# Laying 160 channels as 128 and 32 in a four-layer cross-attention kernel, with the 32-row products issued beside the scores

## The reference

```
q = x @ Wq;  k = ctx @ Wk;  v = ctx @ Wv          # 160 channels = 20 heads x 8
p = softmax(q k^T / sqrt(8))                       # 20 heads, 128 x 77
x = x + (p v) @ Wout + bias
```

## Time and profile before

| | us |
|---|---|
| median of 3 runs | 2361.54 (2361.36 to 2363.28) |
| the profiled execution | 2364.91 |
| its span, first to last instruction | 2363.1 |
| TensorE busy | 2177.9 (92%) |
| TensorE weight loads busy | 1807.6 (76%) |
| VectorE busy | 1397.6 (59%) |
| ScalarE busy | 1076.6 (46%) |
| GpSimd busy | 459.0 (19%) |
| mean granted TensorE clock | 0.968 of full |

### The profile page before, as it was taken

The page is one execution under the profiler, slowest core; times in us unless marked ns, Lnnn a source line. Parts: engine busy times, 40 slices in busy tenths (PEclk is TensorE's granted clock), DMA queues, the critical chain, the costliest instruction groups (busy, mean ns, idle before and its releaser), DMA issues. The chain is left out here.

```text
span 2363.1 us, 74795 instructions
## 1 busy us (share of the span) xinstructions
PE 2177.9 (92%) x26394; PEld 1807.6 (76%) x26394; DVE 1397.6 (59%) x4195; ACT 1076.6 (46%) x2733; POOL 459.0 (19%) x870
## 2 busy tenths in 40 slices
PE   1699999999999999999999999999999999999976
PEld 1578787788788778878878887887878778888765
DVE  3236666566566566656656665665666566566554
ACT  0244444445445444544544454454455445444431
POOL 0012212221121211221212121122122112221210
PEclk9799999999999999999999999999999999999985
DMA  2111111111111111111111111111111111111000
GB/s 85 49 46 37 51 48 36 46 48 44 37 50 43 37 50 49 39 42 49 44 37 50 45 39 46 50 42 40 49 44 37 50 43 42 45 50 35 24 10 5
DMA packets 92280, 101.21 MB, mean 43 GB/s; under 512 B 37313, under 2 KB 68505, under 8 KB 91898
## 3 DMA queue, kind: packets, MB, share of 16 engines
q1 hardware_dynamic: 90220, 92.86, 14.1%
q10 hardware_dynamic: 1678, 3.33, 0.5%
HBM read 34.13 MB, written 5.41 MB: 17 GB/s over the span
## 5 line engine op out<-in xcount | busy, mean ns | idle before, releaser
L1056 DVE TENSOR_REDUCE top<-ps_s 128x6 f32<-128x462 f32 (+3 forms) x1024 | 514.7, 547 | 186.9 <-PE ps_s L687 184.2
L954 ACT ACTIVATE p_t<-ps_s 116x512 f32<-116x512 f32 (+1 forms) x768 | 370.3, 544 | 68.8 <-PE ps_s L714 68.5
L1096 DVE TENSOR_TENSOR weighted<-ps_k,probs 128x462 f32<-128x462 f32 (+1 forms) x256 | 143.2, 559 | 328.7 <-PE ps_k L784 325.2
L687 PE MATMUL ps_s<-k_blocks,q_sb 32*128 32x231 f32 (+1 forms) x3584 | 296.5, 377 | 16.0 <-issue 15.9
L759 PE MATMUL ps_c<-p_t,v_rows 116*27 116x128 f32 (+1 forms) x7168 | 285.0, 282 | 14.2 <-DMA v_rows<-v_img 11.7
L1272 POOL TENSOR_TENSOR k_blocks<-k_sb,mask_k 128x231 f32<-128x231 f32 x384 | 211.6, 572 | 426.5 <-PE ps_s L714 411.5
L759 PEld LDWEIGHTS ps_c<-p_t,v_rows 116*27 116x27 f32 (+1 forms) x7168 | 212.1, 108 | 84.9 <-issue 49.1
L827 PE MATMUL ps_c<-o_t,wo 128*80 128x128 f32 x2048 | 275.4, 278 | 0.5 <-ACT o_t L982 0.5
L982 ACT ACTIVATE o_t<-ps_c 80x256 f32<-80x256 f32 x256 | 97.0, 379 | 336.9 <-PE ps_c L815 238.8
L714 PE MATMUL ps_s<-q_sb,k_blocks 32*116 32x128 f32 (+1 forms) x5376 | 229.2, 286 | 20.3 <-DMA q_sb<-top_t 11.4
L687 PEld LDWEIGHTS ps_s<-k_blocks,q_sb 32*128 32x128 f32 x3584 | 198.0, 185 | 57.9 <-issue 40.7
(11 more groups left out here) (112 smaller groups left out, 2904.6 us busy)
## 6 DMA issues: line engine op xcount, KB each, us to landing
v_rows<-v_img SPq DMA_DIRECT2D x128, 227.4 KB
context<-in_ctx SPq DMA_DIRECT2D x64, 336.0 KB, 3.0
q_sb<-top_t SPq DMA_DIRECT2D x576, 6.0 KB
v_rows<-v_img SPq DMA_DIRECT2D x64, 115.2 KB
v_rows<-v_img SPq DMA_DIRECT2D x64, 112.2 KB
x_in<-in_x SPq DMA_DIRECT2D x64, 80.0 KB, 1.8
out_x<-x_out SPq DMA_DIRECT2D x64, 80.0 KB, 1.7
v_rep<-v_dram SPq DMA_DIRECT2D x64, 50.0 KB
```

The costliest lines, as they stand in the source:

```text
L687: ins = pe.matmul(ps_s[:, z * 512 + j * GT:z * 512 + j * GT + n], q_sb[c % 3][lo:lo + QUAD, j * S:(j + 1) * S], k_blocks[c % 3][lo:lo + QU ...
L954: act.activation(to, source, ACT.Exp, scale=SCALE).then_inc(p_ready, 1)
L1056: dve.tensor_reduce(top[c % 2][:, z * BH:z * BH + m], s.rearrange("p (h t) -> p h t", t=T)[:, :, 0:n], AX.X, ALU.max).then_inc(s_top, 1)
L1096: dve.tensor_tensor(weighted[:, lo * T:hi * T], ps_k[:, 0:(hi - lo) * T], probs[:, lo * T:hi * T], ALU.mult).then_inc(w_ready, 1)
```

## The change

Channels 0 to 127 lie in the first column half of a tile, over all 128 rows; channels 128 to 159 lie in rows 96 to 127 of the second half, the last quadrant. Then:

- `queries` are two products over 128 rows (the *lead*), and `queries_rest` is two products over the 32 rows of the last quadrant. `queries_rest` is issued in `scores`, in the place that the last quadrant leaves empty; the waits of `queries` (for `q_evac`, `top_evac` and x) move there. It starts the accumulation that `queries` ends.
- `project_out` is two products over 128 rows, and `project_rest` is two over 32 rows. These are issued in the two empty places of `exponents`; in step 0, where `second` is `turn`, they stand alone, behind `project_out`. Output channels 32 to 159 are made as the second half, so that the last 32 fall in the last quadrant.
- `project_out` stands ahead of `second` in all steps; before, it stood behind it in steps 0, 1 and 2.
- `turn_image` stands behind `scores`, and in the final step `turn_out` behind `queries`.
- `new_x` is two VectorE instructions (128 x 128, and 32 x 128) that also add the bias from a column, and stands ahead of `weigh(k, t, 1)`. The bias row and the row of ones are gone.
- x is loaded and stored in three transfers instead of one. Loading the weights takes 23 transfers instead of 12, eight of them for the bias columns; eleven tiles are no longer cleared.

```diff
-            def queries(k, c):
+            def queries_rest(k, c):
                 l, b = layer(c), batch(c)
                 pe.wait_ge(q_evac, raised(k, exists, c - 1))
                 pe.wait_ge(top_evac, raised(k, topped, c - 2))
                 if l == 0:
-                    pe.wait_ge(ld_x[b % NX], loads(k, b, NX))
+                    pe.wait_ge(ld_x[b % NX], loads(k, b, NX, per=3))
                 else:
                     pe.wait_ge(x_ready, raised(k, out, c - 5 + LAG))
                 x = x_in[b % NX] if l == 0 else x_work[b % NC]
                 for m in range(2):
-                    for kt in range(2):
-                        ins = pe.matmul(ps_q[:, m * S:(m + 1) * S], w_rows(wq, l, kt, m, 128),
-                                        x[:, kt * S:(kt + 1) * S], start=kt == 0, stop=kt == 1)
+                    pe.matmul(ps_q[:, m * S:(m + 1) * S], q_rows(wq_tail, l, m)[TAIL:LEAD, :], x[TAIL:LEAD, S:2 * S],
+                              start=m == 0, stop=False, skip_group_check=True)
+
+            def queries(k, c):
+                l, b = layer(c), batch(c)
+                x = x_in[b % NX] if l == 0 else x_work[b % NC]
+                for m in range(2):
+                    ins = pe.matmul(ps_q[:, m * S:(m + 1) * S], q_rows(wq_lead, l, m), x[:, 0:S],
+                                    start=False, stop=True, skip_group_check=True)
                 ins.then_inc(q_psum, 1)
...
                         if j >= groups_in(z):
+                            if exists(c + 1):
+                                queries_rest(k, c + 1)
                             continue
...
             def exponents(k, c):
+                t = c + 1
+                if out(t):
+                    pe.wait_ge(ot_evac, raised(k, out, t))
...
                             if j >= groups_in(z):
+                                if out(t):
+                                    project_rest(k, t, kind)
                                 continue
...
             def project_out(k, t):
                 l = layer(out_step(t))
                 pe.wait_ge(ot_evac, raised(k, out, t))
-                for m in range(2):
-                    for kt in range(2):
-                        ins = pe.matmul(ps_c[(t - LAG) % 2][0:HC, m * S:(m + 1) * S], w_half(wo, l, kt, m * HC, HC),
-                                        o_t[:, kt * S:(kt + 1) * S], start=kt == 0, stop=kt == 1)
-                ins.then_inc(y_psum, 1)
+                for j in range(2):
+                    pe.matmul(ps_c[(t - LAG) % 2][:, j * S:(j + 1) * S], o_rows(wo_lead, l, j), o_t[:, 0:S],
+                              start=j == 0, stop=False, skip_group_check=True)
+
+            def project_rest(k, t, j):
+                l = layer(out_step(t))
+                ins = pe.matmul(ps_c[(t - LAG) % 2][:, j * S:(j + 1) * S], o_rows(wo_tail, l, j)[TAIL:LEAD, :],
+                                o_t[TAIL:LEAD, S:2 * S], start=False, stop=True, skip_group_check=True)
+                if j == 1:
+                    ins.then_inc(y_psum, 1)
 
             def step(k, t):
+                if exists(t):
+                    scores(k, t)
+                elif exists(t + 1):
+                    queries_rest(k, t + 1)
                 if ip(out_step(t)):
                     turn_image(k, t)
-                if exists(t):
-                    scores(k, t)
-                if out(t):
+                elif out(t):
                     turn_out(k, t)
                 if exists(t + 1):
                     queries(k, t + 1)
+                if ip(out_step(t)):
+                    turn_out(k, t)
                 if e_values(t):
                     values(k, t)
                 if exists(t - 2):
                     product(k, t - 2)
-                if layer(t) == L - 1 and out(t):
+                if out(t):
                     project_out(k, t)
+                    if not topped(t - 1):
+                        project_rest(k, t, 0)
+                        project_rest(k, t, 1)
                 if e_waves(t):
                     gram_wave(k, t, 0)
                 if topped(t):
@@ -851,8 +918,6 @@
                     second(k, t - 1)
                 if e_waves(t):
                     gram_wave(k, t, 1)
-                if layer(t) != L - 1 and out(t):
-                    project_out(k, t)
...
-                dve.tensor_tensor(to[0:HC, :], ps_c[(t - LAG) % 2][0:HC, 0:2 * S], old[0:HC, :], ALU.add).then_inc(x_ready, 1)
+                y = ps_c[(t - LAG) % 2]
+                dve.scalar_tensor_tensor(out=to[:, 0:S], in0=y[:, 0:S], scalar=bias[:, l:l + 1], in1=old[:, 0:S],
+                                         op0=ALU.add, op1=ALU.add)
+                dve.scalar_tensor_tensor(out=to[TAIL:LEAD, S:2 * S], in0=y[TAIL:LEAD, S:2 * S],
+                                         scalar=bias[TAIL:LEAD, L + l:L + l + 1], in1=old[TAIL:LEAD, S:2 * S],
+                                         op0=ALU.add, op1=ALU.add).then_inc(x_ready, 1)
...
+                if out(t):
+                    new_x(k, t)
                 if e_waves(t):
                     weigh(k, t, 1)
-                if out(t):
-                    new_x(k, t)
```

More of the change, by code:

```diff
@@ L47 @@
 VL = TRI * UC
+LEAD = 128
+TAIL_C = C - LEAD
+TAIL = LEAD - TAIL_C
+CUT_C = LEAD - HC
 NX, NC = 3, 6
@@ L255, in build @@
         x_work = [sb(f"x_work{b}", [128, 2 * S]) for b in range(NC)]
-        x_out = [sb(f"x_out{b}", [HC, 2 * S]) for b in range(NX)]
+        x_out = [sb(f"x_out{b}", [128, 2 * S]) for b in range(NX)]
         context = sb("context", [128, NC * 2 * CX])
@@ L314, in build, with q_rows, o_rows, parts @@
         ps_k = pb("ps_k", [128, 512])
[L317 to L319 removed]
+        def q_rows(w, l, m):
+            at = (l * 2 + m) * 128
+            return w[:, at:at + 128]
+        def o_rows(w, l, j):
+            at = l * C + j * TAIL_C
+            return w[:, at:at + LEAD]
+        def parts(tile, array):
+            return ((tile[0:HC, 0:S], array[:, 0:S]),
+                    (tile[HC:LEAD, 0:S], array[0:CUT_C, S:2 * S]),
+                    (tile[TAIL:LEAD, S:2 * S], array[CUT_C:HC, S:2 * S]))
         def w_rows(w, l, kt, m, n):
@@ L450, in run, with by_row, by_partition @@
                 step(None, t)
-        WEIGHTS = [(wq_in[0:HC, :], a["wq"]), (wo[0:HC, :], a["wo"]), (wk_in[:, :], a["wk"]),
+        def by_row(lead, tail, array):
+            halves = array.rearrange("p (l k n) -> p k l n", l=L, k=2)
+            lead, tail = [w[:, :].rearrange("p (l n) -> p l n", l=L) for w in (lead, tail)]
+            return [(lead[0:HC], halves[:, 0]), (lead[HC:LEAD], halves[0:CUT_C, 1]), (tail[TAIL:LEAD], halves[CUT_C:HC, 1])]
+        def by_partition(l, lo, hi):
+            return a["bias"][0:1, l * 2 * C + lo:l * 2 * C + hi].rearrange("o (p x) -> (o p) x", x=1)
+        BIAS = [p for l in range(L) for p in ((bias[:, l:l + 1], by_partition(l, 0, LEAD)),
+                                              (bias[TAIL:LEAD, L + l:L + l + 1], by_partition(l, LEAD, C)))]
+        WEIGHTS = by_row(wq_lead_in, wq_tail_in, a["wq"]) + by_row(wo_lead, wo_tail, a["wo"]) + BIAS + [
+                   (wk_in[:, :], a["wk"]),
                    (wkip_in[:, :], a["wkip"]), (wv[:, :], a["wv"]), (wvip[:, :], a["wvip"]),
@@ L456, in build, with in_order @@
                    (mask_vip[:, :], a["mask_vip"])]
-        N_SET, N_SET_POOL = 33, 3
+        N_SET, N_SET_POOL = 22, 3
         RUNS = column_runs()
-        N_LD = 16 * (len(WEIGHTS) + 1 + 4 * 4)
-        def in_order(eng, to, source, n, columns):
+        N_LD = 16 * (len(WEIGHTS) + 4 * 4)
+        def in_order(eng, to, source, columns, lo=0):
             t = to[:, :].rearrange("p (a m n) -> p a m n", m=2, n=128)
             f = source[:, :].rearrange("p (a m n) -> p a m n", m=2, n=columns)
-            for (m, lo), (j, at), width in RUNS:
-                eng.tensor_copy(t[0:n, :, j, at:at + width], f[0:n, :, m, lo:lo + width]).then_inc(w_order, 1)
+            for (m, src), (j, at), width in RUNS:
+                eng.tensor_copy(t[lo:128, :, j, at:at + width], f[lo:128, :, m, src:src + width]).then_inc(w_order, 1)
         @block.sync
@@ L481, in next_x @@
                 sp.wait_ge(x_ready, raised(k, out, t - 4 + LAG))
-                sp.dma_start(x_in[b % NX][0:HC, :], of_batch(k, a["x"], b)).then_inc(ld_x[b % NX], 16)
+                for to, source in parts(x_in[b % NX], of_batch(k, a["x"], b)):
+                    sp.dma_start(to, source).then_inc(ld_x[b % NX], 16)
             def store(k, t):
@@ L486, in store @@
                 sp.wait_ge(x_ready, raised(k, out, t))
-                sp.dma_start(of_batch(k, a["out"], b), x_out[b % NX][:, :]).then_inc(st_x[b % NX], 16)
+                for source, to in parts(x_out[b % NX], of_batch(k, a["out"], b)):
+                    sp.dma_start(to, source).then_inc(st_x[b % NX], 16)
             def next_six(k, t):
@@ L981, in results @@
                 act.wait_ge(y_psum, raised(k, out, t - 1))
```

(7 more changed lines are left out.)

31 lines of the change are left out of this document (16 added, 15 removed).

## The result

The changed kernel takes 2299.2 us (median of four runs, 2297.49 to 2301.27), beside 2361.5 for the kernel before on the same chip: ratio 0.9736, 95% interval 0.9719 to 0.9753, so 2.6% faster. I had predicted 2190 in a range of 2158 to 2248. The sign and the mechanism of the quadrants came out, the size did not: 109 us are missing. The profiled execution took 2298.45 with a span of 2296.7.

What follows compares the result with a forecast made beforehand. TensorE's order of records was taken as the time, except where something makes it wait; -2.83 us a cycle times 60.6 gave -171, with -4 and +2 from 2364.9 giving 2192, rounded to 2190 us, range 2158 to 2248.

Steps and rivals of the forecast that it cites:

- What is late next: Part of the prediction pricing each interval between steps, from L815 to L815; its sum was -2.83 us a cycle.
- Steps 1 to 2: Interval from step 1's L815 to step 2's: queries 0.44, project 0.44, L745 0.42 and L800 1.05 saved, -2.35 us.
- Steps 2 to 3: Interval from step 2's L815 to step 3's: queries and project -0.88, turn_image +0.11 and a 0.25 wait, p_ip_t +0.10; -0.42 us.
- L745's wait: Step 1's wait for VectorE's maxima, 0.42 against an unwaited start, claimed to go as maxima run ahead during longer step 0.
- L800's wait: Step 2's wait for o_last ahead of the scores; scores could start at 1215.38 instead of 1216.43, saving 1.05.
- The 0.10 for p_ip_t: In steps 2 to 3, p_ip_t's record, copy and hops take 0.65, of which queries and the record fill 0.55: +0.10.
- Steps 0 to 1: Interval from step 0's L815 to step 1's: 6.45 against 6.07, +0.38, with a new stall of some 0.65 in scores.
- Steps 3 to 0: Interval from step 3's L815 to step 0's: ScalarE's chain only 0.44 earlier by queries, project's 0.44 lost to waiting; -0.44.
- Queries: In each step four of eight query records leave TensorE's path, saving 0.44; rests in scores cost 0, bounds up to 0.64.
- Rests behind the scores: Rival: rests start only behind the scores, each costing 0.25, 1.0 a cycle, 61 us, giving 2250 us; chance 0.13.
- `new_x`: On VectorE, one instruction of 0.42 becomes two, 0 to 0.42 more, taken as 0.15, hidden beside TensorE's turn_back, keys and scores.
- Chains take over: Rival: maxima land late or VectorE's longer `new_x` pushes the image branch, 0.5 a cycle more, 30 us: 2220 us; chance 0.13.

Runs made afterwards that it cites:

- the seventh experiment: Changed kernel with project_out's leads behind the second gram wave and new_x behind the second weighting in steps 1 and 2, image_branch 8 to 15 behind the next maxima: 2238.1 us.
- the fifth experiment: Changed kernel with queries_rest directly ahead of queries, among full-row products, instead of in the last quadrant's empty place: 2486.7 us, ratio 1.054.
- the kernel with order alone: Kernel before, old 80 and 80 channel layout, with the image turned behind the scores and image_branch 8 to 16 done one step later: 2272.7 us, ratio 0.962.

## Why the prediction was wrong, point by point

- **The failed step.** Under "What is late next", in "Steps 1 to 2" and "Steps 2 to 3", I took the output product's 0.44 off and let `keys` follow `turn_back` as before: "keys end at 1214.29 + 1.16 = 1215.45", and "0.22 (L792's two records) + 1.09 (keys, L603)". `keys` writes the bank from which the second weighting reads. The change moves the product away from between the gram wave and `turn_back`, so from the last gram record to `keys` stand 0.33 of records instead of 1.21. The chain needs 0.30 from that record to L1160 and 0.64 for it. Both stood in the rows: L1096 at 1213.40 ends at 1214.04, and L603 starts at 1214.29, with 0.25 to spare while 0.88 of cover was about to go. I followed that weighting to o_last and not to `keys`. Medians from `turn_back` to `keys`: 0.94 and 0.83 where I had 0.22.
- **Steps 1 to 2** came out at 8.92 instead of 8.05: 0.72 by that wait, 0.11 by `keys` itself, which takes 1.20 instead of 1.09 when it has waited, and 0.06 by exponents that take 1.23 where they took 1.17 before. (I listed 1.07 for them, which holds for steps 2 and 3.) Both numbers hang on VectorE's image branch: with its part moved they fall to 1.09 in the seventh experiment and to 1.07 on the old layout. The other terms came in: queries, L745's wait and L800's wait.
- **Steps 2 to 3** came out at 8.88 instead of 8.38: the wait of `keys` 0.61 and `keys` itself 0.10 (1.24 behind a wait, 1.14 before), less the 0.25 for `turn_image`, which did not occur, as the wait of `keys` had met it. The 0.10 for p_ip_t came: the final `turn_out` takes 0.79 and took 0.70. Small terms make the other 0.04.
- **Steps 0 to 1**: 6.68 instead of 6.45. The mechanism was right, with the stall within the scores 1.62 - 0.99 = 0.63 against 0.65. A size was off: lead and rests take 1.28 and not 1.07, since the first record of either form takes 0.21.
- **Steps 3 to 0**: 8.19 against 8.18. The total was right, the place only in part. I let ScalarE's chain, which holds the scores, take the output product's 0.44. It takes 0.09 there (scores 1.45, before 1.37); 0.29 goes ahead of the exponents, to the wait for VectorE's `less_top`: from the lead to the exponents it is 0.93, and 0.64 in the fifth experiment, where that wait isn't hit.
- **The sum.** The four misses are 0.23 + 0.87 + 0.50 + 0.01 = 1.61; times 60.6 cycles, 98 of the 109 us. From the start of the last scores to the end of the span it is 45.5 instead of 41.2, where I had counted on a gain; the remaining few us are not followed up.
- **Queries** went as predicted: half the records gone, the rests free in the scores. The lower bound, 0, was right, and with it falls the rival "Rests behind the scores". Its page, the Trainium skill, TensorE: Matmul & The Clock Gate, The mechanism, has matmuls start in program order. The trace differs: the four L708 records, issued behind all records of the scores, start at 1251.55, 1251.66, 1251.77 and 1251.88, and of the six scores records issued ahead of them one starts at 1251.66 with the second L708, and three as late as 1251.86. The measurement decides.
- **`new_x`** takes 0.35 + 0.36 where one instruction took 0.42: 0.29 more and not 0.15. I called it hidden beside `turn_back`, `keys` and scores; in step 2 it stood ahead of the weighting that `keys` waits for, and costs 0.28 there.
- **"Chains take over"** came nearest (2220): the kind of event was right, a chain of VectorE's, but the two that I named played a small part (the longer `new_x` costs 0.28 in step 2, the image branch 0.06 in the exponents of step 1), and the price was three times as high.
- **Where the 62 us come from.** Turning the image behind the scores gives 60 alone. Moving the product ahead costs 60 alone, on the old layout. If the parts add up, and no run shows that they do, what the layout saves on TensorE was about paid back by that. With the image behind and the branch late in both, the two layouts give 2272.7 and, with the lead behind and full rests in step 0, 2206.6: 66 us for the new layout.

## What to carry to other kernels

When work moves away from between two instructions of an engine, list for every instruction behind the gap what it waits for, and set the idle or the spare of each against the length of the cover that leaves; a wait that the profile does not show may be met by a quarter of a microsecond only. A change made of layout and order should be priced as two: here one move of order alone gave nearly as much as the whole change, and another alone cost as much. And a move that frees one engine may be worth nothing until the queue of the next is cleared: the same move of step 0 lost 11 us with VectorE's branch ahead of the maxima and lost nothing without it.

## What the runs showed of the hardware

- Records in different row quadrants start out of their order of issue (L708 at 1251.55, six records issued ahead of it from 1251.66 on), and four 32-row records of 128 columns cost nothing that shows in the last quadrant's free place: 2298.1 us without them, 2299.2 with them.
- A change of form costs twice, 0.10 ahead of the new form and 0.10 on its first record (0.05 where that is a transpose): the four leads, four rests and `turn_back` of step 0 take 1.55 with 32-row rests and 1.21 when all are products of 128 rows. The Trainium skill, TensorEngine Tiling (Array Packing), Tiling Modes, says only that the change drains the engine; a cost of 0.34 us for two changes agrees with that.
- VectorE's sum of y, bias and x takes 0.35 for 128 x 128 elements and 0.36 for 32 x 128: the time does not fall with the partitions here, so cutting 160 channels as 128 and 32 makes two full prices.
- Eight times in a run, as often as the loop of nine rounds goes back, TensorE stands still for about 2 us ahead of the scores with no releaser shown: 15.9 in all before, 18.1 after, 16.6 in the kernel with order alone. It is in all kernels alike. In the kernel before, TensorE's granted clock fell to the lower level (1.2 GHz) within 1.5 us behind each of them, for 3.4 us (6.8 behind the first); in the changed kernel it did so behind seven of the eight.
